# Summing the four expert rows of each token by identity products on TensorE, in a hybrid attention and mixture-of-experts kernel

## The chip, the cores and the metric

The kernel runs on one core of one Trainium2 chip. The time is that of one launch on the device in microseconds (us). The kernel before took 1328.7 us (median of 3 runs, 1328.54 to 1333.18).

## The reference, cut to what matters

The input x is 4 batches of 512 tokens by 256 features, float32. Four layers follow one another, each on the layer-normalized x and each added to it:

```python
x = x + attn_a(layernorm(x))   # 8 kv heads, groups of 4, rotary positions
x = x + ffn(layernorm(x))      # 16 experts, 4 chosen per token, and a shared one
x = x + attn_b(layernorm(x))   # 32 half heads, differential attention
x = x + ffn(layernorm(x))
# in ffn, for every token t:
y[t] = sum(weight[t, k] * expert[k](xt[t]) for k in the 4 chosen)   # four result rows
return y + shared(xt)
```

## The kernel before, in words

Tokens are handled in 16 tiles of 128, four tiles (`TB`) to a batch, four batches (`B`). Every engine has its own program, written out by hand in order; engines meet through named semaphores only. Names in what follows: PE is TensorE, DVE VectorE, ACT ScalarE, POOL GpSimd, SP the engine that issues most transfers.

An ffn layer ends like this. The weighted result rows of the experts are scattered to a DRAM table `y_rows`, four rows per token. When all are stored, `sp_ffn_back` loads them back in eight transfers of 1 MB, q = 0 to 7, each with two token tiles and four rows per token (`back`: two regions of the arena and one of `y_sb`; the fourth batch uses the first region again, so its two loads wait until the first four tiles are summed). `dve_sum` then makes of them, per q, three VectorE additions: 4 rows to 2 (L1206), 2 to 1 (L1208), and that onto the residual `x_sb` (L1210). After the second ffn, `h`, the eight sums stand at the program's end, each followed by the store of its two tiles.

After the first ffn, `f`, the sums are part of the second attention's projections, its prologue. `dve_prologue` does q0 and q1 first, with the layer-norm statistics (`dve_stats`, L907 and L909), `dve_rstd` and the four normalized tiles of batch 0 (`dve_ln`, L945). Then come for every batch b eight pieces k = 0 to 7, on TensorE `pe_piece`: k = 0 to 2 turns (transposes, L1515) of the normalized tiles and the v products of tiles 0 and 1 (L1535), k = 3 the v products of tiles 2 and 3, k = 4 to 7 the four blocks of q and k (`pe_block`, L1574; 2 products of 512 columns each). ScalarE takes the high part of each block (`act_block`, L749), VectorE the rest (`dve_rest`, L968), and blocks 2 and 3 may only start when the rests of blocks 0 and 1 are taken, since they share two PSUM banks. In k = 0 to 3 VectorE also makes the sums, statistics and `dve_rstd` of the next batch, and in k = 3 and 4 its normalized tiles. From batch 1 on, first score units of the attention stand behind the pieces (`first_units`: 6 with batch 1, 12 with batch 2); each is a maximum on VectorE (L1088), and TensorE's unit i waits for the maximum of unit i-2. `t_ps` and `o_ps` are two PSUM banks used for the turns.

Of the kernel before, what the change touches and what calls it, by code (L numbers as in the profile page):

```python
# [25 lines left out]
TB = T // P  # L26
# [27 lines left out]
TOPK = 4  # L54
# [45 lines left out]
def build(nc, ins, out):  # L100
    ctx = ExitStack()
    with ctx:
# [648 lines left out]
        def act_std(act, k, a, c):  # L751

            act.wait_ge(sm("var"), k)
            act.activation(nw[:, 0, a:c], nw[:, 1, a:c], ACT.Sqrt).then_inc(sm("std"), 1)

        def act_weights(act):

            act.dma_start(wqkv[:, :, 0:448], ins["a_wqkv"].rearrange("(c p) n -> p c n", p=P)).then_inc(sm("a_w"), 16)
            act.dma_start(px_b[:], ins["a_bqk"]).then_inc(sm("a_w"), 16)
            act.dma_start(bv[:], ins["a_bv"].partition_broadcast(P)).then_inc(sm("a_w"), 16)  # L760
            act.dma_start(rot, ins["rot"].rearrange("p (a t) -> p a t", a=2)).then_inc(sm("a_w"), 16)
# [22 lines left out]
        def act_proj_b(act):  # L784
            act_std(act, 5, 0, TB)
            for b in range(B):
                act_tile_T(act, "b", b, 0)
                act_tile_T(act, "b", b, 1)
                for u in range(2):
                    act_v(act, b, u)  # L790
                    act_tile_T(act, "b", b, u + 2)
                act_v(act, b, 2)
                act_v(act, b, 3)
                if b + 1 < B:
                    act_std(act, 6 + b, TB * (b + 1), TB * (b + 2))
                for i in range(BLOCKS["b"]):
                    act_block(act, b, i)
            act.wait_ge(sm("b_lam"), 1)
            act.activation(lam[:, 2:4], lam[:, 0:2], ACT.Exp).then_inc(sm("b_lam_exp"), 1)

# [110 lines left out]
        def dve_rstd(dve, k, section, a, c):  # L911

            ch = straight_chain(dve)
            dve.wait_ge(sm("stats"), NT * section + c)
            dve.tensor_scalar(nw[:, 1, a:c], mv[:, a:c, 1], EPS, None, ALU.add).then_inc(sm("var"), 1)
            dve.wait_ge(sm("std"), k)
            ch(dve.reciprocal(nw[:, 2, a:c], nw[:, 0, a:c]))
            ch(dve.tensor_tensor(nw[:, 3, a:c], nw[:, 2, a:c], nw[:, 2, a:c], ALU.mult))
            ch(dve.tensor_tensor(nw[:, 3, a:c], nw[:, 3, a:c], nw[:, 1, a:c], ALU.mult))  # L920
            ch(dve.tensor_scalar(nw[:, 3, a:c], nw[:, 3, a:c], -0.5, 1.5, ALU.mult, ALU.add))
            ch(dve.tensor_tensor(rstd[:, a:c], nw[:, 2, a:c], nw[:, 3, a:c], ALU.mult))

        def dve_rsqrt(dve, ch, y, v, t):

# [75 lines left out]
        def dve_piece_b(dve, b, k):  # L1001

            if k == 0 and b > 0:
                dve_rest(dve, b - 1, 3)
            if k >= 5:
                dve_rest(dve, b, k - 5)
            if k == 7 and b == B - 1:
                dve_lambda(dve)
            if b + 1 < B and 3 <= k <= 4:
                dve_ln(dve, "b", TB * (b + 1) + 2 * k - 6)  # L1010
                dve_ln(dve, "b", TB * (b + 1) + 2 * k - 5)

        def dve_lambda_sums(dve):
            ch = straight_chain(dve)
# [22 lines left out]
        def dve_prologue(dve, s):  # L1037
            if s == "a":
                dve_x_stats(dve, 0)
                for u in range(TB):  # L1040
                    dve_ln(dve, s, u)
                dve_x_stats(dve, 1)
                dve.wait_ge(sm("consts"), 16)
                dve.wait_ge(sm("a_w"), 64)
            else:
                for u in range(TB):
                    dve_back(dve, u)
                dve_rstd(dve, 5, 2, 0, TB)
                for u in range(TB):
                    dve_ln(dve, s, u)  # L1050
                dve.wait_ge(sm("b_w"), 112)
                dve_lambda_sums(dve)
            for b in range(B):
                for k in range(8):
                    if s == "b" and b + 1 < B and k < TB:
                        dve_back(dve, TB * (b + 1) + k)
                        if k == TB - 1:
                            dve_rstd(dve, 6 + b, 2, TB * (b + 1), TB * (b + 2))
                    if s == "a":
                        dve_piece_a(dve, b, k)  # L1060
                    else:
                        dve_piece_b(dve, b, k)
                    for i in first_units(s, b, k):
                        dve_first_max(dve, s, i)
            if s == "b":
                dve_rest(dve, B - 1, 3)
            dve.wait_ge(sm(s + "_xnT"), NT)
            dve.memset(o_ps[:], 0.0).then_inc(sm("o_init"), 1)
            for i in rest_units(s):
                dve_first_max(dve, s, i)  # L1070
# [111 lines left out]
        def dve_seam(dve, s):  # L1182
# [10 lines left out]
            for i in range(len(NORMS) - 1):  # L1193
# [2 lines left out]
                    dve_out_x(dve, s, t)  # L1196
                dve_seam_rstd(dve, 1 if s == "a" else 3, a, c)

        def dve_sum(dve, f, q):

            b, u, t = q // 2, q % 2 * 2, 2 * q
            done = q + 1 + past(f, 2 * B)
            part = back[b][:, u:u + 2]
            dve.wait_ge(sm(f"load{q}"), 16 * (loads(q) + past(f, loads(q))))
            dve.tensor_tensor(part[:, :, 0:2, :], part[:, :, 0:2, :], part[:, :, 2:4, :], ALU.add).then_inc(sm("back_half"), 1)  # L1206
            dve.wait_ge(sm("back_half"), done)
            dve.tensor_tensor(part[:, :, 0, :], part[:, :, 0, :], part[:, :, 1, :], ALU.add).then_inc(sm("back_sum"), 1)  # L1208
            dve.wait_ge(sm("back_sum"), done)
            dve.tensor_tensor(x_sb[:, t:t + 2, :], x_sb[:, t:t + 2, :], part[:, :, 0, :], ALU.add).then_inc(sm(f + "_x"), 2)  # L1210

        def dve_back(dve, t):

# [291 lines left out]

        def pe_turn(pe, s, b, u):

            t = TB * b + u  # L1510
            pe.wait_ge(sm(s + "_xn"), t + 1)
            if t >= 2:
                pe.wait_ge(sm(s + "_xnT"), t - 1)
            for c in range(CE):
                mm = pe.transpose((t_ps if u % 2 == 0 else o_ps)[:, c * P:(c + 1) * P], xn[:, u, c * P:(c + 1) * P],  # L1515
                                  ident_f)
            mm.then_inc(sm(s + "_xt"), 1)
# [101 lines left out]
        def pe_prologue(pe, s):  # L1619
            for b in range(B):  # L1620
                for k in range(8):
                    pe_piece(pe, s, b, k)
                    for i in first_units(s, b, k):
                        pe_first_scores(pe, s, i)
            for i in rest_units(s):
                pe_first_scores(pe, s, i)
# [390 lines left out]
        @block.tensor  # L2017
        def _(pe):
            pe.wait_ge(sm("consts"), 16)
            pe_attn(pe, "a")  # L2020
            pe_ffn(pe, "a", "f")
            pe.wait_ge(sm("b_w"), 112)
            pe_attn(pe, "b")
            pe_ffn(pe, "b", "h")

# [79 lines left out]
```

## Time and profile before

| | |
|---|---|
| median of the runs | 1328.7 us |
| the profiled execution | 1329.73 us, its span 1327.8 us |
| busy over the span: PE, DVE, ACT, POOL | 86%, 66%, 41%, 43% |
| granted TensorE clock, mean | 0.941 of 2.4 GHz |
| last write of the experts' rows issued to the end | 1295.9 to 1327.8 us |
| the prologue of the second attention | about 645 to 754 us |

### The profile page before, as it was taken

To read this page: it belongs to the slowest core of one execution; us is meant where nothing else is said; L and a number is where in the kernel's file an instruction comes from. 1 tells how busy PE (TensorE), PEld (TensorE's weight loads), DVE (VectorE), ACT (ScalarE), POOL (GpSimd) and SP (SyncE) were. 2 spreads that over 40 slices of the span, in tenths; PEclk is the share of its full clock that TensorE was granted. 3 is DMA by queue.
4 is the path that set the end of the run, shared out by engine and by line. 5 is a ranking of instruction groups with operands and counts; after the bars stand their busy time and mean duration, and the time that the engine had idled before them with its cause. 6 is when DMAs were issued, how large, how long until landed. Compare 5 with 4: busy or idle time off the path is not lost.

```text
span 1327.8 us, 25926 instructions
## 1 busy us (share of the span) xinstructions
PE 1146.8 (86%) x8708; PEld 614.7 (46%) x8708; DVE 876.1 (66%) x1968; ACT 542.1 (41%) x846; POOL 570.0 (43%) x813
## 2 busy tenths in 40 slices
PE   6887999998889999999377799999878999989990
PEld 2343344443565566555243344444337456655550
DVE  5578989992585344444489799999757744444446
ACT  2124777778531122222132377777865112222210
POOL 4452444544125556433333345554540455563340
PEclk9886999999989999999798899999998998999995
DMA  4522111110643455453554422222026235545528
GB/s 137 156 87 97 40 46 41 48 39 3 255 101 112 146 174 168 140 159 112 200 186 138 150 57 57 57 56 58 15 95 201 75 113 171 177 153 150 148 78 324
DMA packets 105650, 156.67 MB, mean 118 GB/s; under 512 B 19440, under 2 KB 81840, under 8 KB 105008
## 3 DMA queue, kind: packets, MB, share of 16 engines
q1 hardware_dynamic: 91760, 117.53, 29.6%
q0 software_dynamic: 13056, 36.46, 7.6%
q8 instruction: 73, 1.20, 0.4%
q10 hardware_dynamic: 704, 1.02, 0.2%
q14 instruction: 57, 0.47, 0.1%
HBM read 97.76 MB, written 58.58 MB: 118 GB/s over the span
## 4 chain that ended last, share of the span: by engine, by line
PE 60%; DVE 21%; ACT 6%; issue 6%; DMA 4%; POOL 2%; SPq 2%; POOLq 0%; DVEq 0%; ACTq 0%
PE pair_ps L1957 10%; PE o_ps L1721 9%; ACT arena L814 4%; DVE nm L1088 4%; PE pair_ps L1899 4%; PE pair_ps L1990 3%; DVE bm L1088 3%; PE t_ps L1747 2%; PE pair_ps L1671 2%; PE pair_ps L1993 2%; PE pair_ps L1552 2%; PE pair_ps L1651 2%; PE pair_ps L1676 2%; PE pair_ps L1646 2%; PE pair_ps L1944 2%
## 5 line engine op out<-in xcount | busy, mean ns | idle before, releaser
L814 ACT ACTIVATE arena<-pair_ps 128x1024 f32<-128x1024 f32 x320 | 322.7, 1025 | 131.1 <-PE pair_ps L1646 76.3
L616 POOL TENSOR_SCALAR_AFFINE_SELECT arena<-arena 128x512 f32<-128x512 f32 (+1 forms) x320 | 174.9, 547 | 240.9 <-ACT arena L814 240.4
L1088 DVE TENSOR_REDUCE nm<-pair_ps 128x2 f32<-128x1024 f32 (+1 forms) x192 | 232.5, 1221 | 32.9 <-PE pair_ps L1695 29.2
L671 POOL DMA_INDIRECT x_slots<-y_sb,slot_i x128 | 124.0, 969 | 193.8 <-DVE slot_i L1291 89.8
L1721 PE MATMUL o_ps<-arena 128*9 128x512 f32 (+7 forms) x2048 | 177.0, 441 | 4.2 <-POOL arena L616 3.9
L1957 PE MATMUL pair_ps<-arena 128*128 x512 | 170.8, 476 | 1.9 <-ACT arena L865 1.9
L1088 DVE TENSOR_REDUCE bm<-pair_ps 128x8 f32<-128x1024 f32 x128 | 155.2, 1216 | 4.2 <-PE pair_ps L1695 1.0
L1436 DVE TENSOR_TENSOR arena<-arena,pair_ps 128x128 f32<-128x128 f32 x144 | 41.3, 287 | 123.6 <-ACT arena L870 123.2
L1957 PEld LDWEIGHTS pair_ps<-arena 128*128 128x128 f32 x512 | 95.3, 198 | 44.5 <-issue 7.5
L1451 DVE TENSOR_SCALAR xnT<-pair_ps,slot_w 128x256 f32<-128x256 f32 x144 | 65.5, 481 | 73.5 <-PE pair_ps L1995 40.4
L870 ACT ACTIVATE arena<-pair_ps 128x176 f32<-128x176 f32 x144 | 45.7, 317 | 147.0 <-PE pair_ps L1957 130.5
L677 POOL DMA_INDIRECT y_f<-xnT,dest x72 | 69.1, 959 | 78.3 <-DVE xnT L1451 62.5
L677 POOL DMA_INDIRECT y_h<-xnT,dest x72 | 69.0, 959 | 78.0 <-DVE xnT L1451 59.2
L1899 PE MATMUL pair_ps<-arena 128*128 128x512 f32 (+1 forms) x192 | 90.0, 612 | 0.0
L1695 PE MATMUL pair_ps<-c_b 64*128 64x128 bf16 (+1 forms) x1280 | 85.5, 211 | 0.0
L1695 PEld LDWEIGHTS pair_ps<-c_b 64*128 64x128 bf16 x1280 | 61.3, 99 | 34.0 <-issue 4.9
L1671 PE MATMUL pair_ps<-arena 48*128 48x512 bf16 x256 | 51.6, 397 | 24.2 <-ACT arena L814 18.4
L1990 PE MATMUL pair_ps<-arena 128*128 x224 | 59.8, 390 | 7.5 <-DVE arena L1444 7.5
L1646 PE MATMUL pair_ps<-arena 51*128 51x512 bf16 x256 | 51.0, 394 | 14.6 <-DVE bm L1088 7.2
L1721 PEld LDWEIGHTS o_ps<-arena 128*9 128x9 f32 (+1 forms) x2048 | 38.9, 93 | 52.8 <-issue 30.5
L861 ACT ACTIVATE sil<-pair_ps 128x512 f32<-128x512 f32 (+1 forms) x24 | 14.3, 595 | 105.1 <-PE pair_ps L1899 105.1
L865 ACT ACTIVATE arena<-t_ps 128x512 f32<-128x512 f32 x36 | 21.5, 597 | 86.1 <-PE t_ps L1932 86.1
(282 smaller groups left out, 2005.9 us busy)
## 6 DMA issues: line engine op xcount, KB each, us to landing
arena<-x_slots SPq DMA_DIRECT2D x128, 134.0 KB, 2.2
arena<-in_w SPq DMA_DIRECT2D x4, 2816.0 KB, 18.5
arena<-q_a SPq DMA_DIRECT2D x64, 96.0 KB
arena<-y_f SPq DMA_DIRECT2D x6, 1024.0 KB, 9.9
arena<-q_b SPq DMA_DIRECT2D x64, 96.0 KB
arena<-y_h SPq DMA_DIRECT2D x6, 1024.0 KB, 10.0
arena<-in_w SPq DMA_DIRECT2D x2, 2048.0 KB, 16.9
arena<-in_w SPq DMA_DIRECT2D x72, 48.0 KB, 2.0
```

The source lines that it names most:

```text
L616: pool.affine_select(p, p, pattern, ALU.is_ge, 0.0, base=0, channel_multiplier=-1)\
L671: pool.indirect_dma_start(x_slots, bass.IndirectOffsetOnAxis(ap=slot_i[:, t, k:k + 1], axis=0), y_sb[:, t, :], None).then_inc(sm(f"scat{n ...
L677: pool.indirect_dma_start(y_rows[f], bass.IndirectOffsetOnAxis(ap=dest[:, j:j + 1], axis=0), yt[:, j % XR, :], None).then_inc(sm(f"store{j ...
L814: act.activation(p_ring[:, U % RING, :], pair_ps[:, pair_at("T", n, u)].rearrange("p a c -> p (a c)"), ACT.Exp, scale=SCALE).then_inc(sm(" ...
L1088: dve.tensor_reduce(dst, src, X, ALU.max, negate=not 2 <= u < 4).then_inc(sm("t_max_done"), 1)
L1646: mm = pe.matmul(ps, k_of(s, g, h, KM, 0, P), q_of(g, h, KM, 0, T), start=True, stop=True, skip_group_check=True)
L1671: pe.matmul(ps, q_of(g, h, KQ, 3 * P, T), k_of(s, g, h, KQ, 0, T), start=True, stop=False, skip_group_check=True)
L1695: mm = pe.matmul(blocks[:, :, 64 * half:64 * half + 64], mask_h[lo:lo + 64, half * P:half * P + P], ident_b[lo:lo + 64, lo:lo + 64].unsque ...
L1721: mm = pe.matmul(o_ps[32 * h:32 * h + vw, T - c:T], v_all[:, g, TB * b + j, v0:v0 + vw], p_ring[:, U % RING, a:a + c], start=j == 0, stop= ...
L1899: mm = pe.matmul(st_ps[0:m, k % 2, 512 * a:512 * a + 512], ws13[:, a, e, r:r + m], xnT_all[:, e, b * T:(b + 1) * T], start=e == 0, stop=e ...
L1957: mm = pe.matmul(s_ps[:, j % 2, 0:2 * INTER], xgT[:, j // 2 % 2, j % 2, c, :], w13[:, c, ds(e, 1), :].rearrange("p a i -> p (a i)"), start ...
L1990: pe.matmul(st_ps[:, h, 512:512 + E], hsT[:, h, :], w2[:, 0, ds(e, 1), :].rearrange("p a d -> p (a d)"), start=True, stop=False, skip_grou ...
```

## The change

The three VectorE additions per q become four float32 products on TensorE (`pe_sum`), each with the 128x128 identity as weights and one of the four rows of two tiles, 512 columns, as moving data, all added up in one bank of PSUM (`t_ps` for even q, `o_ps` for odd), and one VectorE addition of that bank onto `x_sb`. In the second attention's prologue the sums of the next batch move from k = 0 to 3 to k = 3 and 4: on TensorE behind the v products of tiles 2 and 3 and behind block 0. The normalized tiles of batches 1 to 3 are made by ScalarE (`act_ln_b`) between its blocks 1 and 2, with a bias that one new small VectorE instruction makes; its blocks 0 and 1 now stand around the square root. All the rest stays.

```diff
--- before.py
+++ after.py
@@ -753,6 +753,11 @@
             act.wait_ge(sm("var"), k)
             act.activation(nw[:, 0, a:c], nw[:, 1, a:c], ACT.Sqrt).then_inc(sm("std"), 1)
 
+        def act_ln_b(act, t):
+            act.wait_ge(sm("b_xt"), t - TB + 1)
+            act.activation(xn[:, t % TB, :], x_sb[:, t, :], ACT.Identity, bias=nw[:, 3, t:t + 1], scale=rstd[:, t:t + 1])\
+                .then_inc(sm("b_xn"), 1)
+
         def act_weights(act):
 
             act.dma_start(wqkv[:, :, 0:448], ins["a_wqkv"].rearrange("(c p) n -> p c n", p=P)).then_inc(sm("a_w"), 16)
@@ -791,10 +796,16 @@
                     act_tile_T(act, "b", b, u + 2)
                 act_v(act, b, 2)
                 act_v(act, b, 3)
+                act_block(act, b, 0)
                 if b + 1 < B:
                     act_std(act, 6 + b, TB * (b + 1), TB * (b + 2))
-                for i in range(BLOCKS["b"]):
-                    act_block(act, b, i)
+                act_block(act, b, 1)
+                if b + 1 < B:
+                    act.wait_ge(sm("b_rstd"), b + 1)
+                    for u in range(TB):
+                        act_ln_b(act, TB * (b + 1) + u)
+                act_block(act, b, 2)
+                act_block(act, b, 3)
             act.wait_ge(sm("b_lam"), 1)
             act.activation(lam[:, 2:4], lam[:, 0:2], ACT.Exp).then_inc(sm("b_lam_exp"), 1)
 
@@ -920,6 +931,9 @@
             ch(dve.tensor_tensor(nw[:, 3, a:c], nw[:, 3, a:c], nw[:, 1, a:c], ALU.mult))
             ch(dve.tensor_scalar(nw[:, 3, a:c], nw[:, 3, a:c], -0.5, 1.5, ALU.mult, ALU.add))
             ch(dve.tensor_tensor(rstd[:, a:c], nw[:, 2, a:c], nw[:, 3, a:c], ALU.mult))
+            if k >= 6:
+                dve.scalar_tensor_tensor(nw[:, 3, a:c], mv[:, a:c, 0], -1.0, rstd[:, a:c], ALU.mult, ALU.mult)\
+                    .then_inc(sm("b_rstd"), 1)
 
         def dve_rsqrt(dve, ch, y, v, t):
 
@@ -1006,9 +1020,6 @@
                 dve_rest(dve, b, k - 5)
             if k == 7 and b == B - 1:
                 dve_lambda(dve)
-            if b + 1 < B and 3 <= k <= 4:
-                dve_ln(dve, "b", TB * (b + 1) + 2 * k - 6)
-                dve_ln(dve, "b", TB * (b + 1) + 2 * k - 5)
 
         def dve_lambda_sums(dve):
             ch = straight_chain(dve)
@@ -1052,9 +1063,10 @@
                 dve_lambda_sums(dve)
             for b in range(B):
                 for k in range(8):
-                    if s == "b" and b + 1 < B and k < TB:
-                        dve_back(dve, TB * (b + 1) + k)
-                        if k == TB - 1:
+                    if s == "b" and b + 1 < B and 3 <= k <= 4:
+                        dve_back(dve, TB * (b + 1) + 2 * k - 6)
+                        dve_back(dve, TB * (b + 1) + 2 * k - 5)
+                        if k == 4:
                             dve_rstd(dve, 6 + b, 2, TB * (b + 1), TB * (b + 2))
                     if s == "a":
                         dve_piece_a(dve, b, k)
@@ -1196,18 +1208,16 @@
                     dve_out_x(dve, s, t)
                 dve_seam_rstd(dve, 1 if s == "a" else 3, a, c)
 
+        def sum_ps(q):
+
+            return (t_ps if q % 2 == 0 else o_ps)[:].rearrange("p (t e) -> p t e", t=2)
+
         def dve_sum(dve, f, q):
 
 
-            b, u, t = q // 2, q % 2 * 2, 2 * q
-            done = q + 1 + past(f, 2 * B)
-            part = back[b][:, u:u + 2]
-            dve.wait_ge(sm(f"load{q}"), 16 * (loads(q) + past(f, loads(q))))
-            dve.tensor_tensor(part[:, :, 0:2, :], part[:, :, 0:2, :], part[:, :, 2:4, :], ALU.add).then_inc(sm("back_half"), 1)
-            dve.wait_ge(sm("back_half"), done)
-            dve.tensor_tensor(part[:, :, 0, :], part[:, :, 0, :], part[:, :, 1, :], ALU.add).then_inc(sm("back_sum"), 1)
-            dve.wait_ge(sm("back_sum"), done)
-            dve.tensor_tensor(x_sb[:, t:t + 2, :], x_sb[:, t:t + 2, :], part[:, :, 0, :], ALU.add).then_inc(sm(f + "_x"), 2)
+            t = 2 * q
+            dve.wait_ge(sm("back_pe"), t + 2 + past(f, NT))
+            dve.tensor_tensor(x_sb[:, t:t + 2, :], x_sb[:, t:t + 2, :], sum_ps(q), ALU.add).then_inc(sm(f + "_x"), 2)
 
         def dve_back(dve, t):
 
@@ -1505,6 +1515,19 @@
 
 
 
+        def pe_sum(pe, f, q):
+
+            pe.wait_ge(sm(f"load{q}"), 16 * (loads(q) + past(f, loads(q))))
+            if q >= 2:
+                pe.wait_ge(sm(f + "_x"), 2 * q - 2)
+            if f == "f" and q >= 2:
+                pe.wait_ge(sm("b_xnT"), TB * (q // 2 - 1) + 3 + q % 2)
+            rows = back[q // 2][:, q % 2 * 2:q % 2 * 2 + 2]
+            for k in range(TOPK):
+                mm = pe.matmul(sum_ps(q), ident_f, rows[:, :, k, :], start=k == 0, stop=k == TOPK - 1,
+                               skip_group_check=True)
+            mm.then_inc(sm("back_pe"), 2)
+
         def pe_turn(pe, s, b, u):
 
             t = TB * b + u
@@ -1620,6 +1643,8 @@
             for b in range(B):
                 for k in range(8):
                     pe_piece(pe, s, b, k)
+                    if s == "b" and b + 1 < B and 3 <= k <= 4:
+                        pe_sum(pe, "f", 2 * b + k - 1)
                     for i in first_units(s, b, k):
                         pe_first_scores(pe, s, i)
             for i in rest_units(s):
@@ -2019,9 +2044,13 @@
             pe.wait_ge(sm("consts"), 16)
             pe_attn(pe, "a")
             pe_ffn(pe, "a", "f")
+            for q in range(2):
+                pe_sum(pe, "f", q)
             pe.wait_ge(sm("b_w"), 112)
             pe_attn(pe, "b")
             pe_ffn(pe, "b", "h")
+            for q in range(2 * B):
+                pe_sum(pe, "h", q)
```

TensorE's order in batch 0 of the second prologue. `xn` is a normalized tile, `wqkv` the weights, `pair_ps` a projection's bank. Before:

```order
L1515 MATMUL t_ps<-c_f,xn 128x128 x2
L1515 MATMUL o_ps<-c_f,xn 128x128 x2
L1535 MATMUL pair_ps<-wqkv,xnT 128x256 x2
L1515 MATMUL t_ps<-c_f,xn 128x128 x2
L1535 MATMUL pair_ps<-wqkv,xnT 128x256 x2
L1515 MATMUL o_ps<-c_f,xn 128x128 x2
L1535 MATMUL pair_ps<-wqkv,xnT 128x256 x4
L1574 MATMUL pair_ps<-xnT,wqkv 128x512 x8
```

Changed, the same place, beginning with the sums of q0 and q1 (`arena` holds the result rows, `c_f` the identity):

```order
L1527 MATMUL t_ps<-arena,c_f 128x512 x4
L1527 MATMUL o_ps<-arena,c_f 128x512 x4
L1538 MATMUL t_ps<-c_f,xn 128x128 x2
L1538 MATMUL o_ps<-c_f,xn 128x128 x2
L1558 MATMUL pair_ps<-wqkv,xnT 128x256 x2
L1538 MATMUL t_ps<-c_f,xn 128x128 x2
L1558 MATMUL pair_ps<-wqkv,xnT 128x256 x2
L1538 MATMUL o_ps<-c_f,xn 128x128 x2
L1558 MATMUL pair_ps<-wqkv,xnT 128x256 x4
L1527 MATMUL t_ps<-arena,c_f 128x512 x4
L1597 MATMUL pair_ps<-xnT,wqkv 128x512 x2
L1527 MATMUL o_ps<-arena,c_f 128x512 x4
```

Behind the last row stand the six products of blocks 1 to 3. Four sums of four products have come in: two ahead of the turns, one behind the v products, one behind block 0.

VectorE's order at the end of batch 0, from the reciprocal deviation `rstd` on. Before:

```order
L922 TENSOR_TENSOR rstd<-nw 128x4
L945 TENSOR_SCALAR xn<-x_sb,mv,rstd 128x256 x4
L968 TENSOR_TENSOR arena<-pair_ps,arena 128x512 x3
L1206 TENSOR_TENSOR y_sb<-y_sb 128x2x512
L1208 TENSOR_TENSOR y_sb<-y_sb 128x2x256
L1210 TENSOR_TENSOR x_sb<-x_sb,y_sb 128x512
L907 BN_STATS bst<-x_sb 128x6
L909 BN_AGGR mv<-bst 128x2
L968 TENSOR_TENSOR arena<-pair_ps,arena 128x512
```

Changed, VectorE at the same place (L982 is the rest, L1220 the sum's one addition):

```order
L933 TENSOR_TENSOR rstd<-nw 128x4
L935 SCALAR_TENSOR_TENSOR nw<-mv,rstd 128x4
L982 TENSOR_TENSOR arena<-pair_ps,arena 128x512 x4
L1220 TENSOR_TENSOR x_sb<-x_sb,t_ps 128x512
L918 BN_STATS bst<-x_sb 128x6
L920 BN_AGGR mv<-bst 128x2
```

The normalized tiles are gone, the four rests of the blocks stand together, and the next sum is one addition from PSUM. The rests still stand behind `rstd`.

ScalarE's order in the same batch, from the last v copy on. Before:

```order
L730 ACTIVATE arena<-pair_ps 128x8x16
L754 ACTIVATE nw<-nw 128x4
L749 ACTIVATE arena<-pair_ps 128x512 x4
L720 ACTIVATE xnT<-t_ps 128x2x128
L720 ACTIVATE xnT<-o_ps 128x2x128
```

Changed, ScalarE at the same place (L758 makes the normalized tiles):

```order
L730 ACTIVATE arena<-pair_ps 128x8x16
L749 ACTIVATE arena<-pair_ps 128x512
L754 ACTIVATE nw<-nw 128x4
L749 ACTIVATE arena<-pair_ps 128x512
L758 ACTIVATE xn<-x_sb,nw,rstd 128x256 x4
L749 ACTIVATE arena<-pair_ps 128x512 x2
L720 ACTIVATE xnT<-t_ps 128x2x128
```

The square root (L754) has moved behind block 0, and the four normalized tiles stand between blocks 1 and 2.

## Rows read from the trace of the kernel before

**Rows 1.** The page, shares of the chain that ended last, by engine.

```profile
PE 60%; DVE 21%; ACT 6%; issue 6%; DMA 4%; POOL 2%; SPq 2%; POOLq 0%; DVEq 0%; ACTq 0%
```

**Rows 2.** The chain at the end: start us, us, what.

```profile
1298.87 7.64 DMA arena<-y_h
...
1306.53 1.24 DVE arena L1206
```

**Rows 3.** Timeline at the end: start, us, engine, line, operation, count [idle before].

```profile
1303.47 1.22 DVE L1206 TENSOR_TENSOR arena<-arena 128x1024 f32<-128x1024 f32 x1 [9.16 <-DMA arena<-y_h]
...
1319.82 1.22 DVE L1206 TENSOR_TENSOR arena<-arena 128x1024 f32<-128x1024 f32 x1
1321.07 0.69 DVE L1208 TENSOR_TENSOR arena<-arena 128x512 f32<-128x512 f32 x1
...
1322.47 1.22 DVE L1206 TENSOR_TENSOR arena<-arena 128x1024 f32<-128x1024 f32 x1
...
1324.52 0.69 DVE L1210 TENSOR_TENSOR x_sb<-x_sb,arena 128x512 f32<-128x512 f32 x1
```

**Rows 4.** Windows: stretch, length, busy us by engine, granted clock, DMA share, GB/s.

```profile
1293.00:1303.00 10.00, 0.39 (x4) 0.00 (x0) 0.88 (x2) 0.00 (x0) 2.54 (x3) 0.55 0.49 161
1303.00:1328.00 25.00, 0.00 (x0) 0.00 (x0) 20.33 (x24) 0.00 (x0) 0.00 (x0) 0.50 0.96 375
```

**Rows 5.** Timeline, blocks of projection on TensorE, a block's rest on VectorE.

```profile
671.43 3.17 PE L1574 MATMUL pair_ps<-xnT,wqkv 128*128 128x512 f32 x7
...
676.14 3.70 PE L1574 MATMUL pair_ps<-xnT,wqkv 128*128 128x512 f32 x8 [1.54 <-DVE arena L968]
...
678.79 0.69 DVE L968 TENSOR_TENSOR arena<-pair_ps,arena 128x512 f32<-128x512 f32 x1 [2.11 <-ACT arena L749]
...
687.72 3.60 PE L1574 MATMUL pair_ps<-xnT,wqkv 128*128 128x512 f32 x8
```

**Rows 6.** Timeline from the first load's landing to the first block.

```profile
653.81 1.23 DVE L1206 TENSOR_TENSOR arena<-arena 128x1024 f32<-128x1024 f32 x1 [9.18 <-DMA arena<-y_f]
...
659.70 0.69 DVE L1210 TENSOR_TENSOR x_sb<-x_sb,arena 128x512 f32<-128x512 f32 x1
...
661.41 0.18 DVE L909 BATCH_NORM_AGGREGATE mv<-bst 128x2 f32<-128x6 f32 x1
...
663.07 1.38 DVE L945 TENSOR_SCALAR xn<-x_sb,mv,rstd 128x256 f32<-128x256 f32 x4
...
663.63 0.66 PE L1515 MATMUL t_ps<-c_f,xn 128*128 128x128 f32 x2 [19.91 <-DVE xn L945]
```

**Rows 7.** Windows of 1 us in which the clock was low or rose.

```profile
668.00:669.00 1.00, 1.00 (x5) 0.71 (x4) 0.93 (x5) 0.00 (x0) 0.00 (x0) 0.50 1.02 401
669.00:670.00 1.00, 1.00 (x6) 0.92 (x5) 0.97 (x2) 0.81 (x3) 0.00 (x0) 0.82 1.04 418
...
706.00:707.00 1.00, 0.12 (x2) 0.13 (x4) 1.00 (x2) 0.00 (x0) 0.92 (x2) 0.95 0.03 10
...
710.00:711.00 1.00, 1.00 (x16) 0.70 (x16) 0.97 (x2) 0.55 (x3) 0.00 (x0) 0.84 0.46 127
```

**Rows 8.** Windows, from the first turn of each batch to that of the next.

```profile
663.60:679.70 16.10, 14.48 (x41) 8.71 (x42) 12.96 (x34) 5.17 (x16) 3.39 (x4) 0.82 0.51 200
679.70:699.40 19.70, 14.52 (x83) 7.91 (x81) 18.52 (x32) 5.98 (x18) 9.26 (x9) 1.00 0.54 167
699.40:728.40 29.00, 21.00 (x132) 10.74 (x126) 26.05 (x42) 5.67 (x17) 7.65 (x9) 0.88 0.45 142
```

**Rows 9.** Timeline of batch 1: first sum, first turn, a wait, two maxima.

```profile
679.40 1.47 DVE L1206 TENSOR_TENSOR y_sb<-y_sb 128x1024 f32<-128x1024 f32 x1
679.68 0.38 PE L1515 MATMUL t_ps<-c_f,xn 128*128 128x128 f32 x2
...
684.84 1.10 PE L1535 MATMUL pair_ps<-wqkv,xnT 128*128 128x256 f32 x4 [2.69 <-DVE arena L968]
...
693.69 2.36 DVE L1088 TENSOR_REDUCE nm<-pair_ps 128x2 f32<-128x1024 f32 x2 [0.22 <-PE pair_ps L1695]
```

## The prediction, made before the changed kernel ran

> **What bounds the kernel now.** I read the page's chain first, then the chain and the timeline at the two places that the change touches, then the granted clock there. Over the whole launch TensorE holds most of the chain [rows 1], but the sums stand where TensorE waits. At the end the chain goes from the last expert rows through one 7.64 us load to VectorE and stays there [rows 2]. VectorE starts the first sum at 1303.47, when its load has landed; from 1319.82 to the next sum at 1322.47 is 2.65 us, and the last addition starts at 1324.52 and ends at 1325.2 [rows 3]. Eight sums at 2.65 are 21.2 us, and the loads stay just ahead of them at 375 GB/s, 2.8 us for 1.05 MB. TensorE does nothing there, at the lower level of its clock [rows 4].
>
> At the start of the second attention it is the same: two sums, statistics and the deviation on VectorE from 653.81 to 663.07, and TensorE's first turn at 663.63, after 19.9 us of rest [rows 6]. In the prologue that follows the two engines share the work. TensorE is busy 14.5 of 16.1, 14.5 of 19.7 and 21.0 of 29.0 us in batches 0 to 2, idle 14.8 us in all; VectorE is busy 13.0, 18.5 and 26.1 us there [rows 8]. So VectorE is the fuller one in batches 1 and 2, TensorE in batch 0. That is what the change has to pay for or to win.
>
> **What one sum costs on TensorE.** It is four products of 512 float32 columns. A block of the projection has two of the same shape: x7 records take 3.17 us and x8 take 3.60 us, so a record is 0.43 us and a product, two records, 0.86 [rows 5]. A sum is 8 records, 3.42 us at 2.4 GHz and 6.84 at 1.2 GHz, in place of 1.22 + 0.69 + 0.69 us of VectorE [rows 3], of which one addition stays. That addition now reads PSUM; the block's rest of the same size, also from PSUM, took 0.69 [rows 5], so I take 0.7. TensorE pays 3.42 us for 1.91 us saved on VectorE. Where the two follow each other, one sum takes 4.1 us instead of 2.65; where they overlap, the pace is 3.42.
>
> **The clock at the start.** After its long rest TensorE began at 663.63 and was still at 0.50 in 668 to 669; the 0.82 of the next microsecond puts the rise at about 669.4 [rows 6, 7]. That is 5.7 us at half speed, which costs 2.9 us. A second rise came sooner: down at about 706.9, up again at about 710.3, 3.4 us, a cost of 1.7 [rows 7]. I take 2.9 for both idle starts and keep 1.7 and, by doubling that shorter row, 3.4 as bounds.
>
> **The end: +9.2 us.** First products at 1303.5, eight sums at 3.42 are 27.3, the clock 2.9, the last addition 0.7: VectorE is done at 1334.4 instead of 1325.2. The other additions lie beside the next sum's products (the two banks alternate). The loads land every 2.8 us and no longer limit from the second sum on; those of the fourth batch are asked for some 3 us later, after the second sum, but TensorE wants them only 14 us after that. The last store behind it stays as it is. Bounds from the clock: +8.0 to +9.7.
>
> **The entry of the prologue: +3.8 us.** 653.8 + 2 x 3.42 + 2.9 = 663.5 for the second sum; its addition 0.7. Statistics of two tiles take 1.2 us (from 660.4 to 661.6) and the deviation 1.5 (from 661.6 to the first normalized tile at 663.07) [rows 6]: 666.9 against 663.07. The first sum's addition and statistics hide beside the second sum. I expect the clock to be down again at the first turn, since TensorE rests 4 us; if it isn't, some 2.9 us come back.
>
> **Batch 0: +7.6 us.** I count from the first turn. Turns and v products take 7.4 us as before, clock included (663.6 to 671.0, where the blocks start: 671.43 is the first of the last seven of their eight records). Then sum q2 to 10.8, block 0 to 12.5, sum q3 to 15.9, block 1 to 17.6. Blocks 2 and 3 need the rests of blocks 0 and 1, and these stand on VectorE behind the addition and statistics of q3 and the deviation: 15.9 + 0.7 + 1.2 + 1.5 + 0.2 for the new bias = 19.5, rest 20.2. So TensorE waits 2.6 us, longer than the 1.54 that it waited for a rest before [rows 5]. Blocks 2 and 3 end at 23.6; before, the next turns came after 16.1 [rows 8]. ScalarE's four normalized tiles, at some 0.4 us each, end at 21.2, before block 2 is there at 21.9: no cost, unless they take over 0.6 us each.
>
> **Batch 1: +4.0 us.** Before, 19.7 us, of which 2.69 went to a v product that waited for a rest behind the sums [rows 8, 9]; that wait goes, and so does most of the later one for the stacks, whose parts are now ready earlier. What is late next is again TensorE with its sums. Turns and v products 5.3, sum 8.7, block 0 10.4, sum 13.8, block 1 15.5; VectorE gives the rest at 13.8 + 3.6 + 0.7 = 18.1, block 2 ends at 19.8. The first two maxima, 1.13 us each when they follow one another (2.36 for two, less 0.1 [rows 9]), delay the next rest to 21.0, block 3 ends at 22.7, and the last unit, which waits for a maximum, at about 23.7.
>
> **Batch 2: 0.** Here VectorE was busy 26.1 of 29.0 us [rows 8]. It loses two sums' first two additions (3.8) and four normalized tiles (1.4); TensorE gets 6.8 us more. With the same durations, and the maxima again between them, the sums end at 12.1 and 17.6, the deviation at 21.2, the blocks at 28.1 and the last unit at 29.0. Bounds: -3.4, if the dips of the clock (0.88 on average) go, and +6.8, if nothing hides. Batch 3 has no sum and stays.
>
> The sum: 9.2 + 3.8 + 7.6 + 4.0 = +24.6 us on the profiled execution's 1329.7, which is 1 us above the median of the runs; on the median that is 1353.3.
>
> **A rule on the shared memory port.** The first two additions of q4 ran beside GpSimd, and the first took 1.47 instead of 1.22 us [rows 3, 9]. The Trainium skill ("GPSIMD Engine Reference", 1. Specifications) says that GpSimd shares its memory interfaces with VectorE and that they contend where VectorE has two SBUF inputs. By that rule the new addition, with one input in PSUM, wouldn't be slowed; that would give a microsecond or two of VectorE back in batch 1, where the count above has TensorE late, and the sum would stay.
>
> **Rivals.** (a) TensorE's idle time takes in the sums. The prologue's three batches then grow only by 20.5 - 14.8 = 5.7 us, less some 2 for the dips of the clock that vanish: 1328.7 + 9.2 + 3.8 + 3.7 = 1345. For it: VectorE is fuller than TensorE in batches 1 and 2. Against: the sums stand in one piece at one place, and the rests of the blocks still wait behind them.
> (b) The clock falls in the new waits of 2 to 3 us. TensorE's rest of 3.3 us before 706.9 ended at the lower level [rows 7], the one of 2.69 us did not (granted clock 1.00 throughout batch 1) [rows 8, 9]. Each sum then run at 1.2 GHz costs 3.4 more; three of them make 1364.
> (c) Not slower: VectorE was the bound of the prologue and its relief is worth more than the sums. It loses 6 x 1.91 + 12 x 0.35 = 15.7 us in batches 0 to 2 (four normalized tiles took 1.38 [rows 6]). If every one of these counted, 1328.7 - 15.7 + 9.2 + 3.8 = 1326. It decides only from the point where TensorE's 20.5 us of sums fit into its gaps, and these are 14.8 [rows 8].
> (d) The change doesn't cost what it says: products with the identity run in one record each, as the turns do (x2 records for two transposes [rows 9]). Then a sum is 1.7 us, the end is held by its loads and stays, the entry costs 0.9, batch 0 4.1, batch 1 0.6 and batch 2 gives back 3.4: about 1331. Against: these are plain products, and every plain float32 product here has two records. The Trainium skill ("TensorE: Matmul & The Clock Gate", Terms) says that the transpose mode makes float32 four times faster; the sums don't use that mode, so by the rule they get nothing of it.
>
> **The numbers.** Forecast 1353, with 1348 to 1360 as its own range, 60%; (a) 18%; (b) 13%; (c) 4%; (d) 5%. The range 1343 to 1361 leaves out (c), (d) and most of (b). What can be told from no change here is some 0.5%, 6.6 us. Slower by more than that holds the forecast, (a) and (b) and a little of (d): 92%; within it 6%; faster 2%.
>
> **What would show it.** In the changed profile the time from the first result load's landing to the first turn should be 13 to 14 us instead of 9.8, from turn to turn 23 to 24 in batches 0 and 1 and 29 in batch 2; at the end eight groups of 8 records, 3.42 us apart, VectorE mostly idle, and a granted clock that rises 3 to 6 us after their start. A spacing of 2.7 us or less at the end, 4 records per sum, or a batch 0 under 19 us would make it wrong.

## The result, and the profile after

The changed kernel took 1354.46 us (median of 5 runs, 1352.22 to 1364.19), the kernel before 1331.91 us in the same comparison (5 runs, 1328.54 to 1333.18). The ratio is 1.0211, 95% interval 1.0184 to 1.0237: slower, by 24 to 32 us. The forecast was 1353.

Launches of one kernel differ by several microseconds in stretches that the change doesn't touch. The first result load landed at 653.8 us before and at 648.2 after, and between 652.7 and 658.2 in the experiments on kernels that are the same up to there. So I compare stretches inside the profiled executions. They run from the first landing of a result load to the first turn (entry), from each batch's first turn to the next (batch 0, 1, 2), from batch 3's first turn to the first score unit behind the prologue (batch 3; L1646 before, L1671 after), and at the program's end from the first landing to the end of the last addition (end). The prologue is entry and batches together.

Entry and end repeat to 0.4 us, and the changed kernel's prologue, which ran unchanged in two experiments, took 119.0, 119.3 and 119.2. But where the clock fell at other moments, the same code took 98.3 us in one run and 100.9 in another (c_moved_only and g_split_tail below). Differences of up to 2.6 us between two prologues are therefore not told from none.

| us | entry | batch 0 | batch 1 | batch 2 | batch 3 | prologue | end |
|---|---|---|---|---|---|---|---|
| before | 9.8 | 16.1 | 19.7 | 29.0 | 25.3 | 99.9 | 21.7 |
| forecast | 13.6 | 23.6 | 23.7 | 29.0 | 25.3 | 115.2 | 30.9 |
| changed | 13.9 | 23.8 | 25.1 | 31.0 | 25.3 | 119.0 | 31.2 |

The two stretches grew by 19.1 + 9.5 = 28.6 us, which is what the ratio says of the launch (0.0211 x 1331.9 = 28). The profiled spans differ by 24.1 only, since the changed one happened to reach its first landing 5.6 us earlier.

The chain at the end, after the change (start, us, what), answers to [rows 2, 3]:

```profile
1317.34 6.37 PE t_ps L1527 x8
1323.71 3.43 PE o_ps L1527 x8
1327.14 3.43 PE t_ps L1527 x8
...
1344.31 3.45 PE o_ps L1527 x8
...
1347.85 0.69 DVE x_sb L1220
```

VectorE, which held this chain before, is in it for one addition; the rest is TensorE, eight records a sum, 3.43 us each. The first one took 6.37. The windows there (as [rows 4, 7]) say why:

```profile
1317.30:1348.50 31.20, 30.40 (x64) 13.08 (x64) 5.47 (x8) 0.00 (x0) 0.00 (x0) 0.91 0.77 286
1322.00:1323.00 1.00, 1.00 (x2) 0.36 (x2) 0.00 (x0) 0.00 (x0) 0.00 (x0) 0.63 1.01 406
1323.00:1324.00 1.00, 1.00 (x4) 0.40 (x3) 0.18 (x1) 0.00 (x0) 0.00 (x0) 1.00 1.05 422
```

TensorE is busy all the time, at 1.2 GHz until about 1322.7, 5.4 us after its start, and the memory traffic has fallen from 375 to 286 GB/s: the loads no longer press.

The entry of the prologue, timeline, as [rows 6]:

```profile
648.20 6.43 PE L1527 MATMUL t_ps<-arena,c_f 128*128 128x512 f32 x8 [10.04 <-DMA arena<-y_f]
654.47 3.60 PE L1527 MATMUL o_ps<-arena,c_f 128*128 128x512 f32 x8
...
658.17 0.69 DVE L1220 TENSOR_TENSOR x_sb<-x_sb,o_ps 128x512 f32<-128x512 f32 x1 [1.54 <-PE o_ps L1527]
...
662.11 0.66 PE L1538 MATMUL t_ps<-c_f,xn 128*128 128x128 f32 x2 [4.05 <-DVE xn L959]
```

Two sums, one addition, statistics, deviation, first turn, with 4.05 us of rest for TensorE before it. Then batch 0, and from batches 1 and 2 the two blocks that took longest, as [rows 5]:

```profile
674.42 3.60 PE L1527 MATMUL o_ps<-arena,c_f 128*128 128x512 f32 x8
677.85 1.88 PE L1597 MATMUL pair_ps<-xnT,wqkv 128*128 128x512 f32 x4
682.32 3.70 PE L1597 MATMUL pair_ps<-xnT,wqkv 128*128 128x512 f32 x8 [2.59 <-DVE arena L982]
...
704.03 2.93 PE L1597 MATMUL pair_ps<-xnT,wqkv 128*128 128x512 f32 x4 [1.93 <-DVE arena L982]
...
733.63 0.39 PE L1708 MATMUL pair_ps<-arena 48*128 48x256 bf16 x4 [2.15 <-DVE bm L1100]
735.36 3.52 PE L1597 MATMUL pair_ps<-xnT,wqkv 128*128 128x512 f32 x4 [1.22 <-DVE arena L982]
```

The wait of 2.59 us stands where the forecast put 2.6. A block of four records takes 1.9 to 2.0 us at full speed; these two took 2.93 and 3.52, because the clock fell. It didn't fall in the waits ahead of them: block 2 of batch 1 started at 704.03, and the windows put the fall at about 704.9; by the same reading the other fell at about 735.7, 0.3 us after its start.

```profile
704.00:705.00 1.00, 0.97 (x2) 0.49 (x3) 1.00 (x1) 1.00 (x4) 0.88 (x2) 0.97 0.00 0
705.00:706.00 1.00, 1.00 (x3) 0.34 (x1) 1.00 (x2) 0.48 (x1) 0.88 (x1) 0.50 0.00 0
...
735.00:736.00 1.00, 0.64 (x1) 0.30 (x2) 1.00 (x2) 0.00 (x0) 0.61 (x1) 0.83 0.00 0
736.00:737.00 1.00, 1.00 (x3) 0.36 (x2) 1.00 (x2) 0.00 (x0) 0.94 (x1) 0.50 0.00 0
```

By batch, as [rows 8]:

```profile
662.10:685.90 23.80, 21.15 (x57) 11.53 (x58) 7.89 (x26) 7.16 (x20) 3.40 (x4) 0.89 0.19 74
685.90:710.90 25.00, 22.55 (x99) 11.38 (x97) 12.00 (x26) 8.04 (x22) 7.14 (x10) 0.93 0.57 179
710.90:741.90 31.00, 26.36 (x148) 12.85 (x142) 21.03 (x34) 7.67 (x22) 7.46 (x9) 0.94 0.33 102
```

VectorE's busy time fell by 5.1, 6.5 and 5.0 us, TensorE's rose by 6.7, 8.0 and 5.4. The roles have changed: VectorE has slack now and TensorE is the full one, in batch 1 for 22.6 of 25 us.

### The profile page after: what moved, and what is told of

Its sections match the earlier page's. It is cut to its first block, busy times and chain, and to the rows that moved or that the text cites. A ratio compares the mean times of both kernels' runs of the same rounds, so it can differ in the third digit from the quotient of the medians.

```text
span 1351.9 us, 26165 instructions
## 1 busy us (share of the span) xinstructions
PE 1203.3 (89%) x8836; PEld 638.4 (47%) x8836; DVE 840.5 (62%) x1927; ACT 548.1 (41%) x858; POOL 567.0 (42%) x813
## 4 chain that ended last, share of the span: by engine, by line
PE 67%; DVE 17%; ACT 6%; issue 5%; DMA 3%; POOL 1%; SPq 1%; POOLq 0%; ACTq 0%; DVEq 0%
PE pair_ps L1982 10%; PE o_ps L1746 9%; ACT arena L825 4%; PE pair_ps L1924 4%; DVE nm L1100 4%; PE pair_ps L2015 3%; DVE bm L1100 3%; PE t_ps L1527 2%; PE t_ps L1772 2%; PE pair_ps L1696 2%; PE pair_ps L2018 2%; PE o_ps L1527 2%; PE pair_ps L1597 2%; PE pair_ps L1701 2%; PE pair_ps L1676 2%
## 5 line engine op out<-in xcount | busy, mean ns | idle before, releaser
L1100 DVE TENSOR_REDUCE nm<-pair_ps 128x2 f32<-128x1024 f32 (+1 forms) x192 | 232.8, 1222 | 33.0 <-PE pair_ps L1720 28.9
L1671 PE MATMUL pair_ps<-arena 51*128 51x512 bf16 x256 | 51.1, 395 | 14.6 <-DVE bm L1100 7.3
L876 ACT ACTIVATE arena<-t_ps 128x512 f32<-128x512 f32 x36 | 21.5, 597 | 83.2 <-PE t_ps L1957 83.2
## 6 DMA issues: line engine op xcount, KB each, us to landing
arena<-in_w SPq DMA_DIRECT2D x4, 2816.0 KB, 20.5
```

The lines of the kernel that those rows point to most:

```text
L1100: dve.tensor_reduce(dst, src, X, ALU.max, negate=not 2 <= u < 4).then_inc(sm("t_max_done"), 1)
```

## The experiments

Theory 1 is the forecast's: TensorE stands alone on the path at the end and at the entry, and in the prologue the sums lie on TensorE's path, with the rests of the blocks waiting behind them on VectorE. The rivals were that loads pace the end, that the place of the sums and not their engine is the cost, and that VectorE was the bound and gets relief. The launches are too few and too scattered to carry single microseconds: a_tail_dve, e_half, d_warm and j_rest_first stand 13, 11, 9 and 8 us below the changed kernel by their ratios to before, and 7, 5, 1 and 2 us by their medians. The readings rest on the stretches.

**a_tail_dve: the end's sums back on VectorE.**

```diff
-            for q in range(2 * B):
-                pe_sum(pe, "h", q)
 # and for f == "h" dve_sum is the three additions of the kernel before
```

> The changed kernel with the eight sums at the program's end given back to VectorE (three additions each); the prologue stays changed. Theory 1 (the end was bound by VectorE and is now bound by TensorE): from the first load's landing to the last addition 21.7 us as before instead of 31.2, the launch 9.5 us shorter than the changed kernel. Rival (the end waits for its loads in both, the sums are hidden): 31 us stays, the launch within 2 us of the changed kernel.

End 21.66 us, prologue 119.3. Launch 1347.5 us (median; ratio to before 1.0110, interval 1.0089 to 1.0131). Theory 1: the end's 9.5 us are the engine's, to 0.1 us.

**e_half: two of four products at the end.**

```diff
-            for k in range(TOPK):
+            n = TOPK if f == "f" else TOPK // 2
+            for k in range(n):
```

> The changed kernel; at the end only two of the four rows of each token are added (the result lacks the other two). Theory 1 (TensorE is the bound of the end): products halve to 1.7 us per sum, below the pace of the loads, so the sums become paced by their loads at 2.6 to 2.8 us; first landing to last addition 22 to 24 us instead of 31.2, launch 7 to 9 us below the changed kernel. Rival (the transfers or the stores pace the end): less than 3 us.

End 21.14 us, a little below the 22 to 24 expected. The steady part, timeline:

```profile
1336.60 1.98 PE L1528 MATMUL o_ps<-y_sb,c_f 128*128 128x512 f32 x4 [0.58 <-DMA y_sb<-y_h]
...
1339.16 1.98 PE L1528 MATMUL t_ps<-arena,c_f 128*128 128x512 f32 x4 [0.58 <-DMA arena<-y_h]
```

Launch ratio to before 1.0127 (1.0106 to 1.0149). With half the work TensorE waits 0.58 us for every load, and the sums follow each other every 2.56 us. So the loads' pace is 2.56 us, VectorE's before was 2.65, TensorE's is 3.43. Before, the two bounds stood 0.09 us apart; a faster engine could have won about 0.6 us on the pace of seven sums, and beyond that only on the one sum that follows the last load.

**d_warm: TensorE kept at work while it waits for the loads.**

```diff
+        def pe_keep(pe):
+            for _ in range(11):
+                pe.matmul(o_ps[:], ident_f, x_sb[:, 0:2, :], start=True, stop=True, skip_group_check=True)
 # called ahead of the first sum of f and of h
```

> The changed kernel with eleven more float32 products (512 columns, result unused) on TensorE while it waits for the first result load, at the prologue and at the end. Theory 1 (the first sum is slow because the clock is at its lower level after the rest): the granted clock is 1.00 when the first sum starts, that sum takes 3.6 us instead of 6.4, the prologue's entry and the end are 2.8 us shorter each; the turns after the entry stay slow, since TensorE rests 4 us before them. Launch 5 to 6 us below the changed kernel. Rival (the first sum is slow because its load is still arriving or because the loads take the memory): 6.4 us stays, no gain.

```profile
642.48 9.71 PE L1521 MATMUL o_ps<-x_sb,c_f 128*128 128x512 f32 x22
652.71 3.70 PE L1532 MATMUL t_ps<-arena,c_f 128*128 128x512 f32 x8 [0.51 <-DMA arena<-y_f]
...
663.88 0.66 PE L1543 MATMUL t_ps<-c_f,xn 128*128 128x128 f32 x2 [4.04 <-DVE xn L959]
```

The last row's wait is the one for the first normalized tile. The first sum took 3.70 us, entry and end fell by 2.7 us each, to 11.2 and 28.5. That the slow first sum is the clock's is shown. But batches 0 to 2 took 24.4, 23.8 and 32.3, together 0.7 more than in the changed kernel, and they differ by the clock. In batch 0 the wait before block 2 is the same as there, 2.58 us, yet the clock fell about 1.1 us after it and the blocks took 5.40 us instead of 3.70:

```profile
683.09 5.40 PE L1602 MATMUL pair_ps<-xnT,wqkv 128*128 128x512 f32 x8 [2.58 <-DVE arena L982]
...
706.50 1.98 PE L1602 MATMUL pair_ps<-xnT,wqkv 128*128 128x512 f32 x4 [1.93 <-DVE arena L982]
```

In batch 1 it is the other way round: the same wait of 1.93 us, the block behind it at full speed, and the batch took 23.8 us, which is the forecast's 23.7. The stretches are 4.7 us shorter in all; the launch stands at 1.0141 of before (1.0095 to 1.0186).

**j_rest_first: the rest of block 0 ahead of the second sum's addition.**

```diff
                     if s == "b" and b + 1 < B and 3 <= k <= 4:
+                        if k == 4:
+                            dve_rest(dve, b, 0)
                         dve_back(dve, TB * (b + 1) + 2 * k - 6)
 # and not at k == 5 in these batches
```

> The changed kernel with VectorE's rest of block 0 placed ahead of the second sum's addition, statistics and deviation, in batches 0 to 2. Theory 1 (blocks 2 and 3 wait because the rests stand behind the sum): TensorE's wait of 2.6 us before block 2 of batch 0 goes, but block 3 then waits for rest 1, which still stands behind the deviation: net 1.5 to 2 us less in batch 0 and about 1 to 2 in batches 1 and 2 each, 3 to 5 us in all. Rival (TensorE's work alone sets the prologue): under 1 us.

Batches 0 to 2: 22.0, 23.2, 28.3 instead of 23.8, 25.1, 31.0; prologue 112.5, 6.5 us less; launch ratio to before 1.0153 (1.0125 to 1.0180). Of the wait of 2.59 us only this is left:

```profile
687.90 1.98 PE L1599 MATMUL pair_ps<-xnT,wqkv 128*128 128x512 f32 x4 [0.86 <-DVE arena L982]
```

The wait behind the sum is real: batch 0, where the clock stayed up in both kernels at this place, is 1.8 us shorter, as expected. Batches 1 and 2 gave 1.9 and 2.7, but the clock's dips, which cost up to 1.7 us each, are gone from them too, and d_warm shows that a dip can be missing without any edit there. So of the 6.5 us some 3 can be the clock's.

**c_moved_only: the new places and ScalarE's part, no sum on TensorE.**

```diff
-                    if s == "b" and b + 1 < B and 3 <= k <= 4:
-                        pe_sum(pe, "f", 2 * b + k - 1)
 # every pe_sum removed, dve_sum as in the kernel before
```

> The changed kernel with no sum on TensorE at all: VectorE makes the three additions everywhere, but at the new places (pieces 3 and 4), and ScalarE makes the normalized tiles. Theory 1 (TensorE's 3.4 us per sum is what the change costs; the new places and ScalarE's share are a gain or nothing): the prologue from first landing to its end takes 94 to 98 us, under the 99.9 of before and far under the 119.0 of the changed kernel, the end 21.7; launch 2 to 6 us below before. Rival (the later place of the sums is the cost, since the rests of the blocks now stand behind them): prologue over 105 us.

Prologue 98.3, just outside the 94 to 98 expected, end 21.5; batches 15.1, 19.8, 28.3. Launch 1329.9 us, ratio to before 0.9984 (0.9964 to 1.0004), not to be told from it. Against the changed kernel it is 20.7 us less in the prologue and 9.7 at the end. So the sums' engine costs the loss, to within 2.6 us; the 1.6 us by which this prologue is shorter than the one before can't be told from nothing. The rival that the later place is the cost falls. Batch 1 kept its length though: the wait of 2.69 us that I saw there [rows 9] went, and one of 1.60 for a rest came:

```profile
694.53 2.83 PE L1603 MATMUL pair_ps<-xnT,wqkv 128*128 128x512 f32 x4 [1.60 <-DVE arena L982]
```

**l_vector_norms: the normalized tiles back on VectorE.**

```diff
                             dve_rstd(dve, 6 + b, 2, TB * (b + 1), TB * (b + 2))
+                            for u in range(TB):
+                                dve_ln(dve, "b", TB * (b + 1) + u)
 # act_ln_b and the bias taken out
```

> The changed kernel with the normalized tiles of batches 1 to 3 back on VectorE, behind the deviation, four in one piece. Theory 1 (TensorE waits for the rest that stands behind the deviation, so what VectorE does ahead of it counts): each of batches 0 to 2 grows by 1.2 to 1.6 us, the prologue from 119.0 to 123 or 124. Rival (VectorE has slack in the changed kernel, busy share is what counts): under 1 us.

Batches 26.7, 26.4 and 33.1, prologue 125.6, 6.6 us more; launch 1366.9 us, ratio to before 1.0253 (1.0205 to 1.0300). Batch 0 grew by 3.0, twice what the tiles take:

```profile
684.15 1.88 PE L1592 MATMUL pair_ps<-xnT,wqkv 128*128 128x512 f32 x4
...
689.83 5.40 PE L1592 MATMUL pair_ps<-xnT,wqkv 128*128 128x512 f32 x8 [3.80 <-DVE arena L975]
```

The wait is 3.80 us instead of 2.59, and the blocks behind it took 5.40 us instead of 3.70: 1.2 from VectorE, as expected, and 1.7 from the clock, which fell 1 us after the wait. That the longer wait made it fall isn't shown, since in d_warm it fell behind the shorter one. ScalarE's part of the change is a gain, given the rest of it: 6.6 us here, of which the clock made 1.7 in batch 0.

**f_scalar_norms and g_split_tail: can something be won with these parts?** The first leaves the sums at their old places on VectorE; the second is c_moved_only with three of the end's sums on TensorE.

```diff
 # f_scalar_norms, against the kernel before
+                    if s == "b" and k == 0 and b > 0:
+                        dve_rest(dve, b - 1, 3)
                     if s == "b" and b + 1 < B and k < TB:
                         dve_back(dve, TB * (b + 1) + k)
 # g_split_tail, against c_moved_only
+            for q in (1, 3, 5):
+                pe_sum(pe, "h", q)
```

> The kernel before with two edits: normalized tiles of batches 1 to 3 on ScalarE, and the rest of block 3 ahead of the next batch's first sum. All sums on VectorE at their old places. Theory 1: batch 0 loses the 1.4 us of normalized tiles, batch 1 its wait of 2.7 us, batch 2 one to two: prologue 94 to 96 us instead of 99.9, launch some 5 us below before. Rival (the waits only move to another place): under 1.5 us.

> The normalized tiles by ScalarE and the places of the sums as in the changed kernel, all prologue sums on VectorE; at the end sums 1, 3 and 5 are made by TensorE, the other five by VectorE. VectorE then has 15.4 us of work there, TensorE 10.3 plus the slow clock, both under the loads' pace of 2.56 us. Theory 1 (before, the end was set by VectorE's 2.65 us only just above the loads' 2.56): first landing to last addition 20.9 to 21.2 us instead of 21.7. Rival (TensorE's slow first sum, 6.4 us, delays the second one): 22 to 24.

f_scalar_norms: batches 14.8, 20.0, 28.0, prologue 97.9, 2.1 less where 4 to 6 were expected, and within the 2.6 us that can't be told; launch ratio 0.9999 (0.9977 to 1.0021). Batch 1 didn't shrink: the edit only moved its wait, as the rival said. g_split_tail: end 24.4 instead of 21.5, ratio 1.0017 (0.9995 to 1.0040).

```profile
1309.61 5.98 PE L1548 MATMUL o_ps<-arena,c_f 128*128 128x512 f32 x8 [13.19 <-DMA arena<-y_h]
1315.70 0.69 DVE L1241 TENSOR_TENSOR x_sb<-x_sb,o_ps 128x512 f32<-128x512 f32 x1 [6.44 <-PE o_ps L1548]
...
1316.54 3.67 PE L1548 MATMUL o_ps<-arena,c_f 128*128 128x512 f32 x8 [0.94 <-DVE x_sb L1241]
```

VectorE waited 6.44 us for the slow first sum, and since the additions keep their order and TensorE's three sums share one bank, the two engines took turns instead of working side by side. The rival held.

The prologue of g_split_tail has the instructions of c_moved_only in the same order; only a semaphore differs. It took 100.9 us instead of 98.3, batches 15.5, 20.5, 29.7. In batches 1 and 2 the mean granted clock was 0.83 and 0.83, against 0.91 and 0.88 there.

**p_before_warm, n_moved_warm, m_moved_warm_rest: TensorE kept at work ahead of the first turn,** in the kernel before, in c_moved_only, and in that with the rest of block 0 first.

```diff
+            for _ in range(22):
+                pe.matmul(o_ps[:], ident_f, c_f[:, 0:512], start=True, stop=True, skip_group_check=True)
 # behind pe_ffn(pe, "a", "f")
```

> The kernel before with 22 more float32 products (512 columns, result unused) on TensorE in its rest of 19.9 us ahead of the second attention's first turn. Theory 1 (the first turns and v products are slow because of the clock): granted clock 1.00 at the first turn, batch 0 takes 13.3 us instead of 16.1 as long as VectorE's rests don't hold it; VectorE has its rest of block 0 at the same time as before, so most of the gain turns into a longer wait for it: 0 to 1 us. Rival (TensorE's own time sets batch 0): 2.8 us less.

> All sums on VectorE at the changed places, normalized tiles on ScalarE, and the 22 unused products ahead of the first turn. Theory 1: VectorE sets batch 0, so it takes 14.3 to 15.1 us as without the products; prologue 97.5 to 98.5, launch 0 to 3 us below before. Rival: TensorE sets it, prologue 95.5.

> As the one before, with VectorE's rest of block 0 ahead of the second sum in batches 0 to 2. Theory 1: block 2 needn't wait for sums and deviation, the waits of 0.9 and 1.6 us in batches 0 and 1 go and the clock's gain comes through: prologue 93 to 96 us against 99.9 of before and 98.3 without both edits, launch 4 to 6 us below before. Rival (block 3 then waits for rest 1 instead): prologue over 97.

| us | batch 0 | batch 1 | batch 2 | prologue | ratio to before |
|---|---|---|---|---|---|
| p_before_warm | 17.8 | 19.7 | 28.9 | 101.5 | 1.0012 (0.9990 to 1.0034) |
| n_moved_warm | 14.8 | 21.0 | 28.4 | 99.3 | 0.9991 (0.9968 to 1.0013) |
| m_moved_warm_rest | 18.9 | 22.0 | 29.3 | 105.3 | 1.0037 (1.0014 to 1.0060) |

Nothing was won: n_moved_warm's batch 0 is as expected and its prologue not told from that of c_moved_only, m_moved_warm_rest is where its rival put it, and p_before_warm's batch 0 even grew by 1.7 us. Its timeline and clock:

```profile
669.65 3.60 PE L1579 MATMUL pair_ps<-xnT,wqkv 128*128 128x512 f32 x8
...
677.28 5.40 PE L1579 MATMUL pair_ps<-xnT,wqkv 128*128 128x512 f32 x8 [4.04 <-DVE arena L968]
```

```profile
664.00:669.00 5.00, 4.07 (x22) 3.24 (x22) 4.71 (x12) 2.11 (x9) 0.00 (x0) 1.00 1.02 408
...
677.00:679.00 2.00, 1.72 (x2) 0.79 (x3) 0.83 (x2) 0.00 (x0) 1.62 (x2) 0.59 0.00 0
```

The turns ran at full speed, as meant. TensorE then came early to the rest of block 0, which VectorE had no sooner than before; its wait grew from 1.54 [rows 5] to 4.04 us, so that block 2 started 12.5 us after the first turn in both kernels: VectorE sets it. The growth of 1.7 us is the clock's alone: it fell just behind the wait, and blocks 2 and 3 took 5.40 us instead of 3.70. In n_moved_warm the same products lengthened the wait from 0.87 to 2.81 us, and the blocks stayed at full speed:

```profile
678.72 3.70 PE L1608 MATMUL pair_ps<-xnT,wqkv 128*128 128x512 f32 x8 [2.81 <-DVE arena L982]
```

In m_moved_warm_rest the early rest makes VectorE wait for block 0 before it takes up the second sum (2.27 us), that sum's additions, which now lie beside GpSimd, take 3.7 us instead of 2.6, and block 3 waits 5.13 us for the rest of block 1:

```profile
681.80 3.78 PE L1610 MATMUL pair_ps<-xnT,wqkv 128*128 128x512 f32 x4 [5.13 <-DVE arena L982]
```

The same edit that shortened the prologue where TensorE was late made it 6 us longer than n_moved_warm's, where VectorE is. No version beats the kernel before by more than can be told.

## Why the prediction was right, step by step

- **One sum on TensorE, 3.42 us at 2.4 GHz:** 3.43. Every sum has 8 records, so (d), one record per product, is out.
- **The end, +9.2:** +9.5, and a_tail_dve takes it back whole. The clock rose 5.4 us after the start, where 5.7 was taken; d_warm gives 2.7 us for it, where 2.9 was taken. The loads' own pace is 2.56 us and not 2.8; the sum doesn't use it.
- **The entry, +3.8:** +4.1, the 4 us of rest ahead of the turn included, and the clock was low again at the turn, as expected.
- **Batch 0, +7.6:** +7.7 (23.75 instead of 16.05), with the wait of 2.6 us where it was put; j_rest_first and c_moved_only confirm both halves, the wait and the sums.
- **Batch 1, +4.0:** +5.3. Mis-sized by the clock: I counted block 2 at full speed, and behind its wait it took 2.93 instead of 2.0; the units after it were slow too. In d_warm, with the clock at 1.00 in this batch, it took 23.8, as forecast.
- **Batch 2, 0:** +2.0. Mis-sized: the block at 735.36 ran mostly at 1.2 GHz, 3.52 instead of 2.0, which is 1.5 of the 2.0. The score unit's wait of 2.15 us for a maximum behind the deviation stands in j_rest_first too, where the batch took 28.3; whether it costs the rest is open. Rival (b) had put a price on the clock: 10.2 us for three sums at 1.2 GHz. In the changed kernel's batches no sum ran slow; two blocks did, for some 3 us in all.
- **ScalarE's tiles:** they take 0.59 us each, 2.07 for the row of four, not 0.4 each; in batch 0 they ended 0.57 us before ScalarE took up block 2, so they cost nothing, as said, by a small margin.

The whole: 24.6 forecast, 28.6 in the stretches, so the size was some 4 us short, 3.3 of them in batches 1 and 2. That the median came within 2 us of the forecast is partly luck: the launches of before stood 3 us higher in the second comparison than in the first, and the medians are 22.6 us apart where the ratio says 28.

Rival (a), idle time takes in the sums, gave 3.7 us for batches 0 to 2 and is refuted: they took 15.0. Rival (c), relief of VectorE, is refuted by c_moved_only: the same places and the same ScalarE work with no sum on TensorE are 30 us faster than the changed kernel and not told from the one before. The rule of the Trainium skill on the shared memory port ("GPSIMD Engine Reference", 1. Specifications) could not be tried on the new addition: GpSimd never ran beside it in the changed kernel's prologue. All of them took 0.69 us. But a block's rest has the same shape and one input in PSUM too. Before, all three additions of q4 lay beside GpSimd and took 1.47, 0.98 and 1.46 us instead of 1.22, 0.69 and 0.69 (the forecast named two); the changed kernel's rest at 736.35 lay beside GpSimd and took 0.68. That agrees with the rule.

```profile
681.41 1.48 POOL L590 TENSOR_TENSOR arena<-arena 128x512 bf16<-128x512 f32 x1
681.98 1.46 DVE L1210 TENSOR_TENSOR x_sb<-x_sb,y_sb 128x512 f32<-128x512 f32 x1
```

```profile
736.06 1.15 POOL L590 TENSOR_TENSOR arena<-arena 128x512 bf16<-128x512 f32 x1
736.35 0.68 DVE L982 TENSOR_TENSOR arena<-pair_ps,arena 128x512 f32<-128x512 f32 x1
```

## What to carry to other kernels

Adding rows with identity products is no free ride for TensorE: price it by the records of a float32 product of that width (here 3.43 us for what three VectorE additions do in 2.65), and ask first whether the place is one in which TensorE sits idle and comes in cold. Where two engines hand work to and fro, count the path through both; the engine with the higher busy share need not be the one that it pays to relieve: in the changed kernel TensorE is the fuller one, and VectorE's tiles still cost time (l_vector_norms). An edit that only brings TensorE sooner to a wait that another engine ends wins nothing. And compare one prologue with another only beyond what the clock's dips do to the same code, here 2.6 us; one dip makes 1.7 us.

## What the runs showed of the hardware that I had not expected

The clock fell behind waits, but the length of the wait alone doesn't decide whether it does. These are the waits before block 2 of batch 0 and the time of blocks 2 and 3 behind them, without j_rest_first and m_moved_warm_rest, which have other orders there:

| wait, us | blocks 2 and 3, us | in |
|---|---|---|
| 0.9 to 1.5 | 3.70 | before, c_moved_only, f_scalar_norms, g_split_tail |
| 2.58, 2.59 | 3.70 | changed, a_tail_dve, e_half |
| 2.58 | 5.40 | d_warm |
| 2.81 | 3.70 | n_moved_warm |
| 3.80, 4.04 | 5.40 | l_vector_norms, p_before_warm |

The waits of 1.93 us in batch 1 were followed by a block in 2.93, 2.82 and 2.87 us (changed, a_tail_dve, e_half) and in 1.98 (d_warm). In every slow case of batch 0 the clock was still 1.00 when TensorE took up work again, and fell 0.1 to 1.1 us later. What decides it, these runs don't show.
